# Splitting q and k inside PSUM, and an output bias that opens its bank: attention and routed experts on one core

## The reference

```
x = x + attention(layernorm(x))      # 16 heads of 8 channels, causal softmax, biases on qkv and on the output
x = x + experts(layernorm(x))        # 8 experts, the two best by x @ Wg per token; each is
                                     # layernorm * w + b, 128 -> 512, gelu, 512 -> 128, times gate and alpha
```

## Time and profile before

| | us |
|---|---|
| median of 3 runs | 552.31 (552.04 to 553.75) |
| the profiled execution | 551.1 |
| its span, first to last instruction | 549.3 |
| PE busy | 469.0 (85%) |
| DVE busy | 366.3 (67%) |
| POOL busy | 368.2 (67%) |
| ACT busy | 327.2 (60%) |

### The profile page before, as it was taken

The page is one execution under the profiler, slowest core; times in us unless marked ns, Lnnn a source line. Parts: engine busy times, 40 slices in busy tenths (PEclk is TensorE's granted clock), DMA queues, the critical chain, the costliest instruction groups (busy, mean ns, idle before and its releaser), DMA issues.

```text
span 549.3 us, 11776 instructions
## 1 busy us (share of the span) xinstructions
PE 469.0 (85%) x3264; PEld 276.4 (50%) x3296; DVE 366.3 (67%) x1284; ACT 327.2 (60%) x694; POOL 368.2 (67%) x712
## 2 busy tenths in 40 slices
PE   3479999999999999999999999788991999999820
PEld 1135343453453453453453444367881888888820
DVE  4588878899899899899899997641633442222216
ACT  2137787786686686786777677753540555555510
POOL 5956685687987987987987968855565445454520
PEclk9779999999999999999999999898996899999975
DMA  2323133233233233234224212376852695666339
GB/s 63 93 82 86 58 96 117 65 105 106 85 99 118 85 96 119 83 97 123 80 79 121 66 43 84 101 232 196 271 183 73 219 271 186 201 194 197 120 134 332
DMA packets 52727, 70.83 MB, mean 129 GB/s; under 512 B 11063, under 2 KB 38430, under 8 KB 52662
## 3 DMA queue, kind: packets, MB, share of 16 engines
q1 hardware_dynamic: 47478, 59.19, 35.6%
q0 software_dynamic: 4320, 8.53, 4.4%
q10 hardware_dynamic: 864, 2.36, 1.2%
HBM read 36.49 MB, written 20.94 MB: 105 GB/s over the span
## 4 chain that ended last, share of the span: by engine, by line
PE 59%; DVE 11%; POOL 11%; issue 7%; DMA 6%; another core or an unknown queue 3%; ACT 2%; SPq 1%; ACTq 0%; POOLq 0%; DVEq 0%
PE slots L750 10%; PE acc_bank L759 10%; PE acc_bank L691 9%; PE slots L659 9%; PE slots L676 7%; POOL probs L1266 3%; PE misc L627 3%; POOL z_dram L1249 3%; DVE masked L961 2%; DMA y_in<-y_dram 2%; PE misc L613 2%; PE slots L655 2%; PE slots L742 2%; PE misc L706 2%
## 5 line engine op out<-in xcount | busy, mean ns | idle before, releaser
L829 ACT ACTIVATE probs<-slots 128x512 f32<-128x512 f32 (+1 forms) x352 | 182.7, 562 | 67.3 <-PE slots L676 52.9
L961 DVE CUSTOM_DVE_ANT_0 masked<-slots,causal_row 128x512 bf16<-128x512 f32 (+1 forms) x256 | 147.1, 616 | 15.4 <-PE slots L659 15.3
L1266 POOL TENSOR_SCALAR_AFFINE_SELECT probs<-probs 128x128 f32<-128x128 f32 (+2 forms) x352 | 118.2, 355 | 37.5 <-ACT probs L829 32.8
L659 PE MATMUL slots<-stack_k,stack_q 125*128 125x256 bf16 (+3 forms) x512 | 128.1, 306 | 13.2 <-DMA stack_q<-parts 6.0
L676 PE MATMUL slots<-stack_q,stack_k 128*128 128x256 bf16 (+3 forms) x503 | 122.3, 300 | 1.9 <-DMA stack_q<-max_rows 1.7
L1296 POOL DMA_INDIRECT y_dram<-y,z_in x71 | 69.8, 983 | 72.8 <-DVE y L1140 56.0
L859 ACT ACTIVATE hidden<-slots,w_in 128x256 f32<-128x256 f32 (+1 forms) x156 | 63.0, 455 | 77.2 <-PE slots L750 35.1
L691 PE MATMUL acc_bank<-probs,v 128*32 128x512 f32 (+3 forms) x1024 | 95.6, 446 | 3.4 <-POOL probs L1266 2.8
L659 PEld LDWEIGHTS slots<-stack_k,stack_q 125*128 125x128 bf16 x512 | 47.9, 99 | 67.3 <-DVE row_max L961 27.0
L1249 POOL DMA_INDIRECT z_dram<-z,pos x64 | 63.6, 994 | 20.8 <-issue 13.9
L750 PE MATMUL slots<-hdnT,w_in 128*128 128x256 f32 (+1 forms) x312 | 70.8, 371 | 2.7 <-issue 2.7
(11 more groups left out here) (169 smaller groups left out, 527.2 us busy)
## 6 DMA issues: line engine op xcount, KB each, us to landing
w_in<-in_wpack SPq DMA_DIRECT2D x39, 516.0 KB
o_dram<-oT SPq DMA_DIRECT2D x32, 256.0 KB, 2.2
stack_k<-parts SPq DMA_DIRECT2D x95, 64.0 KB
stack_q<-parts SPq DMA_DIRECT2D x93, 64.0 KB
z_in<-z_dram SPq DMA_DIRECT2D x32, 132.0 KB
xt<-in_x SPq DMA_DIRECT2D x8, 256.0 KB, 3.0
onT<-o_dram SPq DMA_DIRECT2D x8, 256.0 KB
o_inv<-inv_dram SPq DMA_DIRECT2D x8, 256.0 KB
```

Of the source, the lines that this page charges most:

```text
L659: mm = pe.matmul(cols[:, i, :], q[0:K1, hh, blk * P:blk * P + P], k[0:K1, hh, 0:w], start=len(heads) == 1, stop=True, skip_group_check=True)
L829: act.activation(probs_of(n), columns(n, slot), ACT.Exp, scale=SCALE).then_inc(s_exp, 1)
L961: dve.tensor_tensor_reduce(out=masked[:, n % MASKED, 0:w], in0=slots[:, slot, 0:w], in1=causal_row[:, T - w:T], scale=1.0, scalar=NEG, op0 ...
L1266: pool.affine_select(out=diag, in_=diag, compare_op=ALU.is_ge, fill=0.0, base=0, pattern=[[0, len(heads)], [1, P]], channel_multiplier=-1) ...
```

## The change

For batches 1 to 7 `q` and `k` have no steps of their own any more. Three steps `part` for each take their place: PE forms q in `misc` in float32 (step 0), and in steps 1 and 2 multiplies the part just read by minus the identity in bf16 and adds it onto the same bank. After each step ACT reads the bank with the bias and rounds it to the next part. POOL's subtractions of these batches are gone, and SP's copies wait on `s_free` for the read of the part. In `project_out` a first bf16 matmul, of ones by three rows that hold the parts of `bp_s`, opens the bank and the projection is added to it; `residual` is gone. The three rows are made once by `bias_parts` on POOL. The tables change, those of the back and the route only for batches 0 to 5.

```
-FRONT = {"ln_stats": 0, "ln_agg": 4, "xnT": 10, "q": 11, "k": 14, "v": 32}
+FRONT = {"ln_stats": 0, "ln_agg": 3, "xnT": 10, "v": 34}
+PART_AT = ((17, 18, 21), (29, 30, 33))
-SPLIT = ((12, 13, 15, 16), (19, 23, 29, 30))
-FIRST_HALF = ((13, 15, 26), (27, 28, 32))
-SECOND_HALF = ((25, 40, 37), (30, 38, 39))
-GROUP = {"max_parts": 11, "maxT": 16}
-BACK = {"residual": 40, "o_load": 48, "o_invert": 57, "o_spread": 61, "o_scale": 65, "proj": 67}
-LAST_BACK = {"residual": 40, "o_load": 45, "o_invert": 56, "o_spread": 61, "o_scale": 65,
+FIRST_HALF = ((12, 23, 24), (30, 36, 28))
+SECOND_HALF = ((26, 29, 25), (33, 37, 41))
+GROUP = {"max_parts": 12, "maxT": 16}
+BACK = {"o_load": 50, "o_invert": 58, "o_spread": 62, "o_scale": 65, "proj": 68}
+LAST_BACK = {"o_load": 45, "o_invert": 56, "o_spread": 61, "o_scale": 65,
-ROUTE = (("r_stats", 101), ("r_agg", 103), ("r_root", 103), ("r_z", 110), ("zT", 112),
-         ("gate", 114), ("r_top", 115), ("r_exp", 117), ("r_copy", 114), ("r_comb", 119),
-         ("rank", 123))
+ROUTE = (("r_stats", 102), ("r_agg", 104), ("r_root", 104), ("r_z", 108), ("zT", 111),
+         ("gate", 113), ("r_top", 114), ("r_exp", 118), ("r_copy", 113), ("r_comb", 120),
+         ("rank", 124))
...
-    at(33, "bias")
+    at(37, "bias")
+    at(38, "bias_parts")
...
# SP, stack_up
-                wait(sp, s_split[i], split_no[("split", b, i, PART_STEP[part])] + 1)
+                if b == 0:
+                    wait(sp, s_split[i], split_no[("split", b, i, PART_STEP[part])] + 1)
+                else:
+                    wait(sp, s_free, misc_no[("part", b, i, part)] + 1)
...
# PE
+            def part(b, i, step):
+                claim(("part", b, i, step))
+                if step == 0:
+                    mm = pe.matmul(misc[:, :], wqkv_s[:, i, :], xnT[:, :], start=True, stop=True)
+                else:
+                    pe.wait_ge(s_neg, 1)
+                    mm = pe.matmul(misc[:, :], minus_b[:, :], parts[:, i, step - 1, :], start=False, stop=True,
+                                   skip_group_check=True)
+                mm.then_inc(s_fill, 1)
...
             def project_out(b):
                 claim(("proj", b))
+                pe.wait_ge(s_wp, 48)
+                wait(pe, s_bias, 1)
+                pe.matmul(misc[:, :].rearrange("p (n c) -> p n c", c=C), row_ones[:, :], bp_rows[:, :, :].broadcast_to([P, NT, C]),
+                          start=True, stop=False, skip_group_check=True)
                 wait(pe, s_on, b + 1)
-                pe.wait_ge(s_wp, 48)
                 for n in range(NT):
                     mm = pe.matmul(misc[:, n * P:n * P + P], onT[:, n * P:n * P + P], wp_s[:, :],
-                                   start=True, stop=True)
+                                   start=False, stop=True, skip_group_check=True)
...
# ACT
+            def part(b, i, step):
+                wait_filled(act, ("part", b, i, step))
+                if step == 0:
                     for half in range(2):
                         act.wait_ge(s_stack[i][(b - 1) % 2][half], 16 * PRODUCTS * ((b - 1) // 2 + 1))
+                act.activation(parts[:, i, step, :], misc[:, :], ACT.Identity, bias=bqk_s[:, i:i + 1]).then_inc(s_free, 1)
...
# DVE, project_out
-                wait(dve, s_resid, b + 1)
...
# POOL
             def init_blank():
+                link(pool.memset(minus_b[:, :], 0.0))
+                pool.affine_select(out=minus_b[:, :], in_=minus_b[:, :], compare_op=ALU.not_equal, fill=-1.0,
+                                   base=0, pattern=[[-1, P]], channel_multiplier=1).then_inc(s_neg, 1)
...
-            def split(b, i, step):
-            def residual(b):
+            def bias_parts():
+                wait(pool, s_free, misc_no[("bias",)] + 1)
+                link(pool.memset(row_ones[:, :], 0.0))
+                link(pool.memset(bp_rows[:, :, :], 0.0))
+                link(pool.tensor_copy(bp_parts[:, 0, :], bp_s[:, :]))
...
+                for m in range(PARTS):
+                    row = slice(32 * m, 32 * m + 1)
+                    link(pool.memset(row_ones[row, :], 1.0))
+                    last = pool.tensor_copy(bp_rows[row, 0, :], bp_parts[row, m, :])
```

More of the change, by code:

```diff
@@ L102, in build @@
         for i in range(2):
-            for step in range(4):
-                at(n + SPLIT[i][step], "split", b, i, step)
             for part in range(PARTS):
+                at(n + PART_AT[i][part], "part", b, i, part)
                 at(n + FIRST_HALF[i][part], "stack", b, i, part, 0)
@@ L146, in build @@
     at(26, "init_wide")
-    at(33, "bias")
-    MISC = ("xnT", "q", "k", "v", "bias", "maxT", "proj", "zT", "gate", "rank")
+    at(37, "bias")
+    at(38, "bias_parts")
+    MISC = ("xnT", "q", "k", "part", "v", "bias", "maxT", "proj", "zT", "gate", "rank")
     schedule, unread = [], []
@@ L270, in build @@
         bp_s = sb("bp_s", [P, P])
+        bp_parts = sb("bp_parts", [P, PARTS, C], BF16)
+        bp_rows = sb("bp_rows", [P, 1, C], BF16)
+        row_ones = sb("row_ones", [P, P], BF16)
+        minus_b = sb("minus_b", [P, P], BF16)
         wg_s = sb("wg_s", [P, E])
@@ L388, in build @@
         s_on = sem("s_on")
-        s_resid = sem("s_resid")
+        s_bias = sem("s_bias")
         s_ratio = sem("s_ratio")
@@ L392, in build @@
         s_sel, s_pos, s_copy, s_table = sem("s_sel"), sem("s_pos"), sem("s_copy"), sem("s_table")
+        s_neg = sem("s_neg")
         s_blank, s_rows, s_ends = sem("s_blank"), sem("s_rows"), sem("s_ends")
@@ L770, in _ @@
             walk({"xnT": turn_xn, "q": lambda b: project(b, 0, "q"), "k": lambda b: project(b, 1, "k"),
-                  "v": project_v, "bias": bias, "pass1": pass1, "pass2": pass2, "pv": pv, "maxT": turn_max,
+                  "part": part, "v": project_v, "bias": bias, "pass1": pass1, "pass2": pass2, "pv": pv, "maxT": turn_max,
                   "proj": project_out, "zT": turn_normal, "gate": gate, "rank": rank,
@@ L793, in biased, with split @@
                 wait_filled(act, (name, b))
-                if b > 0:
-                    wait(act, s_split[i], split_no[("split", b - 1, i, 3)] + 1)
                 act.activation(qk32[:, i, :], projected(b, name), ACT.Identity, bias=bqk_s[:, i:i + 1]).then_inc(s_free, 1)
-            def split(b, i, step):
-                if step == 0 and b > 0:
+            def part(b, i, step):
+                wait_filled(act, ("part", b, i, step))
+                if step == 0:
                     for half in range(2):
                         act.wait_ge(s_stack[i][(b - 1) % 2][half], 16 * PRODUCTS * ((b - 1) // 2 + 1))
+                act.activation(parts[:, i, step, :], misc[:, :], ACT.Identity, bias=bqk_s[:, i:i + 1]).then_inc(s_free, 1)
+            def split(b, i, step):
                 if step == 0:
@@ L871, in _ @@
             walk({"warm": warm, "y_load": load_y, "xnT": turn_xn, "maxT": turn_max, "v": put_v, "q": lambda b: biased(b, 0, "q"), "k": lambda b: biased(b, 1, "k"),
-                  "split": split, "stack": stack_up, "pass2": pass2, "pv_out": pv_out,
+                  "part": part, "split": split, "stack": stack_up, "pass2": pass2, "pv_out": pv_out,
                   "zT": lambda b: copy_misc(("zT", b), zT[:, :]),
@@ L933, in split @@
             def split(b, i, step):
-                if step % 2 == 1 and b == 0:
+                if step % 2 == 1:
                     wait(dve, s_split[i], split_no[("split", b, i, step)])
@@ L1251, in dispatch @@
                                         in_=z[:, b % 2, j, n, :], in_offset=None).then_inc(s_disp[b % 2], 16)
[L1253 to L1259, removed]
             def pass2(n):
@@ L1302, in _ @@
             walk({"init_masks": init_masks, "init_stacks": init_stacks, "init_second": init_second, "init_v": init_v, "init_experts": init_experts,
-                  "init_blank": init_blank, "init_wide": init_wide, "dispatch": dispatch, "turn_y": turn_y, "ln_agg": rsqrt, "r_root": rsqrt_two, "split": split, "max_parts": split_max,
-                  "pass2": pass2, "residual": residual, "r_exp": second_gate})
+                  "init_blank": init_blank, "init_wide": init_wide, "dispatch": dispatch, "turn_y": turn_y, "ln_agg": rsqrt, "r_root": rsqrt_two, "max_parts": split_max,
+                  "pass2": pass2, "bias_parts": bias_parts, "r_exp": second_gate})
 NAMES = ("x", "wqT", "wkT", "wvT", "bq", "bk", "bv", "wpT", "bp", "wg", "alpha", "wpack")
```

9 lines of the change are left out of this document (5 added, 4 removed).

## The result

The changed kernel takes 567.45 us (median of 5 runs, 564.58 to 568.34) where the one before takes 552.24 (5 runs, 551.00 to 553.75): a ratio of 1.0266 with the interval 1.0236 to 1.0297. It is slower by about 15 us. The profiled execution is the quickest of the five, 564.58 us with a span of 562.8, so its trace has to explain 13.5 us against the span of 549.3.

A forecast was written before the change was run, and what follows sets the result against it. PE bounds the kernel, busy 85% of the span. Start +2.5, period without routing +2.6, five steady batches +6.5 and last batch -0.8 give +10.8 on 551.1: 561.9, stated as 562 us, own range 557 to 569, 8-in-10 range 547 to 569.

The forecast's parts named there:

- The wait at tick 44: At the next batch's first pass1, PE waits for k's copies queued on SP: 2.1 us (1.8 to 2.9) a batch.
- The row maxima: Their store, last in SP's queue, lands at 12.6 against 11.0 for pass2 of tick 46: 1.6 us wait even with quicker copies.
- rival 3: Gains and costs cancel, with a tick-44 wait of 1 us in place of 2.1: 553.5 us, chance 0.07.
- the five steady batches: Batches with routing beside them go from 41.47 to 42.8 us each: 5 x 1.3 = +6.5 us (3 to 12).
- Up to the first edge: Start up to tick 44 of batch 0, with v and the projection's bias moved behind tick 34: +2.5 us (1 to 4).
- The set-up: Some 20 small POOL operations (minus_b, bias parts) in the first batch, 5 us: costs nothing, up to 1 us if pv waits.
- The period without routing: First whole batch period, with no routing beside it, goes from 36.4 to 39.0 us: +2.6 (2 to 4).
- PE alone needs 40.8 a batch: Steady batch without SP's wait: 41.47 less 2.7 of closed holes, plus 1.1 of added products and 0.9 of waits.
- small waits: PE waiting for the previous part's read (ticks 17, 18, 30), plus 0.4 for DVE: 0.9 us a batch.
- The last batch and the tiles: Last batch has no front and loses POOL's bias add from its chain; expert tiles follow their start: -0.8 us (-2 to +0.5).
- Rivals 2 and 4: 2: PE's additions cost fully, DVE holes return, 560, chance 0.07. 4: small waits vanish while SP holds PE, 556.5, chance 0.10.
- Rival 1: SP isn't what PE waits for; PE's own work sets the batch, -0.7 to -1.3 us each: 546.5 us, chance 0.27.

The follow-up runs named there:

- first experiment: Changed kernel with the copy of k's third part, half 0, placed at tick 34 in place of 28: 550.28 us, ratio 0.9958.
- second experiment: Changed kernel with the copy of k's second part (part 1 half 0) moved from tick 36 to 31, third part left at 28: 566.35 us, ratio 1.0249.
- mended kernel: The kernel of the first experiment: changed kernel with the copy of k's third part, half 0, at tick 34 in place of 28; 550.28 us, ratio 0.9958.
- bias alone: Kernel before with only the bias part of the change (bias_parts at tick 38, bias matmul, residual gone): 550.75 us, ratio 0.9962.
- split alone: Changed kernel with k's third part at tick 34 and the bias part undone (residual on POOL at tick 40): 550.28 us, ratio 0.9945.
- seventh experiment: Mended kernel with POOL given back four unneeded 128x512 subtractions a batch at ticks 13, 16, 23, 30: 561.97 us, ratio 1.0179.

## Why the prediction was right, and where it wasn't

I forecast 562 us, slower, within 557 to 569 for this case. The time was 567.45: right side, right mechanism, 5 us short, and inside the range by 1.6.

- **The wait at tick 44.** Forecast: SP stands 5 us, ten issues and a store take 7.1, landing 2.5, PE waits 2.1 (1.8 to 2.9), 13 to 16 us in all. Measured at edge 5: 5.64; 7.29 (215.80 to 223.09); 2.25 and 0.14 to PE's start, so 2.4; 2.17; 15.1 in seven. The last k copy's path from its release is 9.72 us against a forecast of 9.6. The rule of the Trainium skill that I named there ("DMA: Bandwidth & Descriptors", anatomy of one DMA: the semaphore wait stands on the issuing sequencer) agrees with the row at 215.80, and the first experiment shows that it decides the time.
- **The row maxima.** I had them leave 1.6 us if the copies were quicker. The second experiment measures 1.95. The two chains are nearly equally long, so rival 3, which needed both to be short, was further off than its 0.07 said.
- **The step that was too small: the five steady batches, 5 x 1.3 = +6.5.** They cost +8.2 (215.44 us against 207.22). Without the low clock they would be 5 x 42.5, +5.3; I had 42.8. The three with it add 2.9. The sum had no term for what a stand of 2 us does to the products behind it. No stand of that kind occurs in a steady batch before, where the clock is 1.00, but the same trace has one after the last edge, with the same fall behind it, so the term could have been seen:

```profile
350.03 0.64 PE L691 MATMUL acc_bank<-probs,v 128*32 128x256 f32 x8 [2.47 <-POOL probs L1266]
```
```profile
350.00:360.00 10.00, 9.18 (x77) 5.00 (x78) 4.82 (x27) 6.95 (x13) 6.70 (x15) 0.83 0.55 173
```

- **The profiled execution and the others.** The median of the runs is 2.9 above the profiled execution. The mean clock of those other runs is 0.933 to 0.942 against its 0.950, which could be the low clock at more edges. It does not show it: the mended kernel's profile has 0.940 over the whole run with no low clock at any edge. Where those 2.9 us arise stays open.
- **Up to the first edge: +2.5 forecast, +2.75 measured, with errors that cancel.** I had tick 34 0.2 late and the stretch behind it at 10.4 in place of 8.1. Measured, pass1 of tick 34 starts 0.5 early (45.56 against 46.10), and from there to the edge it is 11.0 in place of 7.7, 3.3 more: 2.1 from the wait, the rest work moved there (v, and the bias product of tick 37). The set-up that I had at nothing to 1 doesn't show. The first edge of the experiments is no measure of this wait: they have it 1.87 (bias alone), 2.07 (mended) and 2.46 (split alone) late without the wait, but all three have the low clock behind the stand at 39 to 40 us, which neither the kernel before nor the changed one has there.
- **The period without routing:** +2.6 forecast, +2.93 measured, with an edge at the low clock in it.
- **PE alone needs 40.8 a batch.** Measured 40.4. Of the 0.9 for small waits 0.2 us in four batches is left in the mended kernel. Without them my sum would be 39.9, so the gain from the closed holes or the price of the additions was 0.5 too kind. DVE's product of the gates (L1049, L1026 before) went from the 876 ns of the earlier trace rows to 161, as forecast, though it takes only one half of the change to do it (above):

```profile
L1049 DVE TENSOR_TENSOR gates<-gates,second x8: 161/161/164, 128.4 to 417.7; 128x4 f32<-128x4 f32 x8
```

- **ACT.** The read took 694 ns where I took 687, nothing on the path:

```profile
L823 ACT ACTIVATE parts<-misc,bqk_s 128x512 bf16<-128x512 f32 x42 | 29.2, 694 | 14.3 <-PE misc L641 11.6 <-PE misc L644 2.0
```

- **The last batch and the tiles:** -0.8 forecast, -0.4 measured, and that agreement is luck. The last batch itself, from edge 7 to its last product of probs and v, takes 0.9 longer (61.73 against 60.83 us, with the low clock at the edge in it), where I had it shorter; what follows, mostly the tiles, which I had unchanged, takes 1.3 less (189.8 against 191.1). The profiled executions of the other versions have 189.9 to 194.0 there with the same tile code, so this part differs by more than the term; why is open.
- **Rivals 2 and 4.** 2 needed DVE's debt to stay, and in the mended kernel PE waits for DVE 0.2 us in four batches. 4 is half true: the small waits vanish, but where SP holds PE the batch still takes 42.5, not 41.9.
- **Rival 1 as a number.** Its 546.5 is the mended kernel, which gives 550.28. Its steady gain of 1.0 a batch was there (1.05), but the start took 2.1 in place of 0.5, 1.2 of it by the low clock. The profiled executions also differ by 3.2 us behind the last edge (255.1 us against 251.9). Of these 1.0 is in the last batch, where PE now waits 1.08 us for z at 315.74, as it does in every version with the split and the tick 34, and not before, in the changed kernel or with the bias alone. The other 2.2 are in the tiles, where the clock was low for 3.4 us more around 376 us; one pair of traces can't say whether that is the change's.

The signs of the two large terms were both right: POOL's relief gains more than PE's additions cost, and SP's queue eats it several times over. The seventh experiment prices the four subtractions, with the ticks tuned to their absence, at 2.1 us in a steady batch; I had counted on 1.1 for DVE.

## What to carry to other kernels

When an issue is moved ahead of the moment at which its data exist, count everything that the same queue holds behind it up to the next thing an engine needs: here one copy asked for at tick 28, six ticks before its data were read out, cost 3% and turned a gain of 0.4% into a loss. Price a new wait on PE as the wait and what it may do to the clock, and look in the windows right behind it. When a wait ends on a transfer, try the next entry of that queue in thought before moving the one that is named.

## What the hardware showed that I had not expected

Behind a stand of PE of about two microseconds the granted clock fell to 1.2 GHz for 3.4 us, while PE was working again, and then came back. PE had been busy through the whole batch ahead of it, and then stood 2.38, 2.36, 2.17 and 2.10 us; at the three edges without it the stands were 1.92, 2.01 and 2.12. The length of the stand alone does not decide: in the second experiment the clock fell behind stands of 1.95, 2.01 and 2.18 us and not behind 1.67, 1.74, 2.04 and 2.08. With stands of 3.3 to 4.2 us it fell at all seven edges, for up to 6.8 us. With spare products in the gap it fell at none. Each fall cost the changed kernel about 1.0 us net, where the wait had cost a batch 2.1 (42.5 against 40.4). The Trainium skill ("TensorE: Matmul & The Clock Gate", what's actually happening) has the clock follow how busy PE has been recently. The trace agrees as far as it goes: the falls come behind stands, and with the gap filled there were none in seven.
